# Attention b: weighted values in quadrants and in two parts, with copies and exponentials in another order

## The chip, the cores and the metric

The kernel runs on one core of a Trainium2 chip. The metric is device time of one execution in microseconds (us), the median of three runs. PE is TensorE, DVE VectorE, ACT ScalarE, POOL GpSimd.

## The reference, cut to what matters

Four layers with residuals: attention a, a mixture of experts (FFN), attention b, and the FFN again. Inputs are 8 batches of 256 positions by 128 features, all in float32. The change is in attention b:

```
Q, K, V = per head (16 heads of 64) from the normalised x
scores  = Q K^T, masked so that a query sees only keys up to itself
attn    = softmax(scores / 8)
z       = attn V            # the weighted values
out     = z_flat W_O^T      # x = x + out
```

## The kernel before, in words

Attention b goes in 32 steps of one software pipeline: 8 batches with 4 steps each (j = 0 to 3), each step two pairs of heads (x = 0, 1; in a pair hh = 0, 1). A pair is two heads of 64, so q and k of a pair fill 128 partitions. Every engine runs its own `step(b, j)`; order is fixed by hand in the code, and engines wait for each other by semaphores. In step n = (b, j), with n1 the next step and n2 the one behind it:

- PE (`step` in `tensor`): scores of n1 for both pairs (`scores_b`), transposes of the weights of n (`turn_p(n, 0)`), q and k of n2 (`project_qk(n2, 0)`), V (`project_v`), `turn_p(n, 1)`, `project_qk(n2, 1)`, some work for the next FFN layer (`turn_v`, `affinity`, `rank`), at j = 1 the next batch's input turned (`turn_xb`), at j = 0 the output projection of the last batch (`out_proj_b`), and weighted values of n (`values_b`).
- DVE: copy of the values out of PSUM (`copy_z`), reciprocal of the softmax sums (`invert(n, 1)`), maxima of n1's scores (`max_b`, four to a pair, which also write the masked scores to SBUF), copies of q and k (`copy_qk`), a copy of transposed weights (`copy_p`), `invert(n1, 0)`, and small work for the FFN layer.
- ACT: copies of transposed weights (`copy_p`, three of the four that a step has), exponentials (`exp_b`), a copy of V (`copy_v`).
- POOL: multiplies the exponentials by the reciprocals (`divide`).

PSUM is `ps`, 8 banks of 512 columns. Banks 0 to 3 hold the scores, `jb` (bank 4) q and k of a projection, `bank[0]` and `bank[1]` (5, 6) the transposed weights, `bank[2]` (7) V and the weighted values. The queries of the second 128 stand in swapped halves of 64 (`QUERIES`), so that score matmuls on both column halves of PE are nearly even. Such a matmul has 64 rows (one head) and 64 columns (64 queries) of the array: a quadrant. A values matmul before the change has all 128 rows (keys) and 64 columns:

```
last = nc.tensor.matmul(bank[2][hh * DHB:(hh + 1) * DHB, x * L + kt * P:(x + 1) * L],
                        vb[:, v:v + DHB], pT[:, c:c + L - kt * P], start=kt == 0,
```

In the profile L1007 is scores, L1040 `turn_p`, L965 `project_qk`, L972 `project_v`, L1053 `values_b`, L982 `out_proj_b`, L956 `turn_xb`; on DVE L1454 `copy_z`, L1478 `invert`, L1468 `max_b`, L1449 `copy_qk`, L1458 `copy_p`; on ACT L696 `exp_b`, L704 `copy_p`, L709 `copy_v`. A float32 matmul shows as two records. An exponential or maximum shows as the instruction and a read of its accumulator.

Of the kernel before, what the change touches and what calls it, by code (L numbers as in the profile page):

```python
# [48 lines left out]
QUERIES = ((0, 1), (3, 2))  # L49

# [43 lines left out]
def constants():  # L94
# [6 lines left out]
    k = np.arange(L)  # L101
    for t, at, n in ((0, C_CAUSAL, P), (1, C_LATE, L)):
        q = HALF * np.array(QUERIES[t])[r // HALF] + r % HALF
        c[:, at:at + n] = np.where(k[None, :n] > q[:, None], MASKED, 0.0)
# [57 lines left out]
def hybrid_layer(nc, x_in, w_a, wo_a, b_a, bo_a, w_b, wo_b, cent, w1, w2, b2, sel_in, const, out):  # L162
    ctx = ExitStack()
    with ctx:
# [6 lines left out]
        def sems(prefix, names):  # L171
# [115 lines left out]
        (b_w, b_xn, b_xT, b_xTs, b_j, b_qk, b_vp, b_v, b_s, b_mx, b_e, b_r, b_n, b_t, b_pa, b_pd, b_pv,  # L287
         b_z, b_o, b_x) = sems("b_", "w xn xT xTs j qk vp v s mx e r n t pa pd pv z o x")
# [21 lines left out]
        jb = wide[:, 4 * 512:5 * 512]  # L310
        wb_ = [wide[:, i * 512:(i + 1) * 512] for i in range(5)]
        aff_at = ((2 * 512, 6 * 512, 2 * 512, 6 * 512), (5 * 512, 5 * 512, 5 * 512, 0, 2 * 512))
# [245 lines left out]
        def _(act):  # L558
# [81 lines left out]
            def turned_v(k, g):  # L640
                act.wait_ge(f_vT, k * NG + g + 1)
                need(act, f_aff, k * NG + g)
                n = GROUPS[k][g][1]
                nc.scalar.copy(vTt[:, 0:n * P], bank[k][:, 0:n * P]).then_inc(f_vTs, 1)
# [45 lines left out]
            def exp_b(n, x, heads=(0, 1)):  # L690
                act.wait_ge(b_mx, 2 * nth(n) + x + 1)
                for hh in heads:
                    for t in range(T):
                        o, m = p_at(n, x, hh, t), m_at(n, x) + t * 2 + hh
                        px = pb[:, o:o + (t + 1) * P]
                        last = nc.scalar.activation(px, px, ACT.Exp, bias=nmax[:, m:m + 1], scale=-1.0, accum_out=psum[:, m:m + 1])  # L696
# [3 lines left out]
            def copy_p(n, x, hh):  # L700
# [3 lines left out]
                nc.scalar.copy(pT[:, c:c + BLOCKS * P], bank[hh][:, 0:BLOCKS * P]).then_inc(b_pa, 1)  # L704
# [6 lines left out]
            def step(b, j):  # L711
                n, n1 = (b, j), at(b, j + 1)
                bv = b + j // 2
                if ok(n):
                    copy_p(n, 0, 1)
                    copy_p(n, 0, 0)
                if ok(n1):
                    exp_b(n1, 0, [0])
# [4 lines left out]
                if ok(n1):  # L723
                    exp_b(n1, 0, [1])
# [17 lines left out]
        def _(pe):  # L742
# [105 lines left out]
            def turn_v(k, g):  # L848
# [3 lines left out]
                for i in range(n):  # L852
                    t = lo + i
                    last = nc.tensor.transpose(bank[k][:, i * P:(i + 1) * P], pack[:, t * ROW:t * ROW + D], ident)
# [97 lines left out]
            def turn_xb(b):  # L952
                pe.wait_ge(b_xn, b + 1)
                need(pe, b_pa, 3 * STEPS * b - 6)
                for t in range(T):
                    last = nc.tensor.transpose(bank[1][:, t * P:(t + 1) * P], xn[:, t * D:(t + 1) * D], ident)  # L956
                last.then_inc(b_xT, 1)

            def project_qk(n, x):
                need(pe, b_qk, 2 * nth(n) + x)  # L960
                if n[1] == 0:
                    pe.wait_ge(b_xTs, n[0] + 1)
                for i in range(2):
                    c = i * HB * DHB + (2 * n[1] + x) * P
                    last = nc.tensor.matmul(jb[:, i * L:(i + 1) * L], wb[:, c:c + P], xnT[:, 0:L], start=True, stop=True)  # L965
# [20 lines left out]
            def out_proj_last(lo, hi):  # L986

                pe.wait_ge(b_qk, 2 * NB * STEPS)
                pe.wait_ge(b_z, NB * STEPS - STEPS + (hi + 1) // 2)
                for p in range(lo, hi):  # L990
                    for t in range(T):
                        last = nc.tensor.matmul(jb[:, t * P:(t + 1) * P], zT[:, p * L + t * P:p * L + (t + 1) * P],
# [5 lines left out]
            def scores_b(n, x):  # L998
# [3 lines left out]
                for t in range(T):  # L1002
                    for half, q in enumerate(QUERIES[t]):
                        for hh in range(2):
                            rows, n = slice(hh * DHB, (hh + 1) * DHB), (q + 1) * HALF
                            c = (2 * x + hh) * 512 + t * P
                            last = nc.tensor.matmul(wide[half * HALF:(half + 1) * HALF, c:c + n],  # L1007
                                                    qk[rows, r + q * HALF:r + (q + 1) * HALF],
                                                    qk[rows, r + L:r + L + n],
                                                    start=t == 0, stop=t == T - 1, skip_group_check=True)  # L1010
                if x == 1:
                    last.then_inc(b_s, 1)

            def turn_p(n, x):
                pe.wait_ge(b_n, 2 * nth(n) + x + 1)
                for hh in (1, 0):
# [19 lines left out]
                    for c in range(BLOCKS):  # L1036
                        o = p_at(n, x, hh, c)
                        to = bank[hh][:, 0:P] if c == 0 else \
                            view(wide, (5 + hh) * 512 + c * P + HALF, [[-HALF, 2], [1, HALF]])
# [3 lines left out]
            def values_b(n):  # L1043
                pe.wait_ge(b_pa, 3 * nth(n) + 3)
                pe.wait_ge(b_pd, nth(n) + 1)
# [543 lines left out]
```

## Time and profile before

| | us |
|---|---|
| median of 3 runs | 521.23 (521.12 to 521.76) |
| profiled execution, whole | 525.47 |
| its span | 523.7 |
| busy in the span: PE, DVE, ACT, POOL | 433.5, 360.2, 264.8, 237.9 |
| attention b, about | 190 to 449 in the span |

Busy time says how long an engine had something running. Which engine sets the time of a stage is read from who waits for whom there; an engine's idle time costs nothing as long as others don't wait for it. The chain of the profile is followed back from the last instruction.

### The profile page before, as it was taken

The page shows a single profiled execution, that of the slowest core. Times are in us where ns is not written, and L with a number is a line of the kernel's source. Part 1 is how long each engine was busy: PE and PEld are TensorE (multiplying, and loading weights), DVE is VectorE, ACT ScalarE, POOL GpSimd, SP SyncE. Part 2 cuts the span into 40 slices and gives each one's busy share as a digit, 9 for nine tenths or more (in the row PEclk, how much of TensorE's full clock was granted, in tenths as well). Part 3 has the DMA queues.
Part 4 walks back from the last instruction along what each step waited for, and adds up shares of the span by engine and source line. Part 5 has one row for each costly group of instructions (what it writes and reads, how often), then busy time and mean ns, then how long its engine had stood idle before and what let it go on. Part 6 is the DMA issues. An engine that isn't in the chain of part 4 may idle for free.

```text
span 523.7 us, 11678 instructions
## 1 busy us (share of the span) xinstructions
PE 433.5 (83%) x3890; PEld 340.8 (65%) x3890; DVE 360.2 (69%) x1417; ACT 264.8 (51%) x928; POOL 237.9 (45%) x251
## 2 busy tenths in 40 slices
PE   2847989622999388999999999999999998439993
PEld 1324557522999346777787777777787787339992
DVE  6689996723656358867768688786878766446661
ACT  1641036500545127767758678576774857115450
POOL 6100789452445415533436335473455546314453
PEclk9997899555999879999999999999999999759997
DMA  8999930024655200000000000000000000136640
GB/s 313 363 393 421 420 144 0 32 91 121 200 172 160 63 29 1 3 1 1 3 1 3 2 2 11 12 22 1 2 12 11 22 1 22 42 101 199 199 139 5
DMA packets 22234, 48.98 MB, mean 94 GB/s; under 512 B 3328, under 2 KB 13574, under 8 KB 19744
## 3 DMA queue, kind: packets, MB, share of 16 engines
q1 hardware_dynamic: 18880, 40.86, 22.2%
q0 software_dynamic: 3296, 7.39, 4.5%
q8 instruction: 32, 0.52, 0.4%
q14 instruction: 26, 0.21, 0.2%
HBM read 24.99 MB, written 24.15 MB: 94 GB/s over the span
## 4 chain that ended last, share of the span: by engine, by line
PE 62%; DVE 13%; POOL 9%; issue 6%; DMA 4%; ACT 3%; another core or an unknown queue 2%; POOLq 0%; SPq 0%; DVEq 0%; ACTq 0%
PE ps L965 9%; PE ps L909 8%; PE ps L922 7%; PE ps L1040 7%; PE ps L1053 7%; PE ps L1007 6%; PE ps L972 4%; PE ps L982 4%; POOL sum L468 3%; POOL vT L531 2%; PE ps L755 2%; ACT vT L696 2%; DVE prod L1151 2%; POOL sum L476 1%
## 5 line engine op out<-in xcount | busy, mean ns | idle before, releaser
L531 POOL TENSOR_TENSOR vT<-vT,prec 128x256 f32<-128x256 f32 (+1 forms) x128 | 103.2, 827 | 128.3 <-DVE prec L1478 127.3
L696 ACT ACTIVATE vT<-vT,nmax 128x128 f32<-128x128 f32 (+1 forms) x256 | 113.4, 449 | 12.0 <-DVE nmax L1468 11.9
L1468 DVE CUSTOM_DVE_ANT_0 vT<-ps,cst 128x128 f32<-128x128 f32 (+1 forms) x256 | 77.5, 350 | 6.8 <-PE ps L1007 6.7
L704 ACT COPY prod<-ps 128x384 f32<-128x384 f32 x96 | 42.9, 482 | 60.5 <-PE ps L1040 60.5
L965 PE MATMUL ps<-xnT,wb 128*128 128x256 f32 x256 | 67.3, 386 | 1.4 <-DVE qk L1449 0.9
L1040 PEld LDWEIGHTS ps<-cst,vT 128*128 128x128 f32 x384 | 42.8, 141 | 30.2 <-issue 16.7
L1040 PE MATMUL ps<-cst,vT 128*128 128x128 f32 x384 | 54.5, 278 | 4.0 <-POOL vT L531 2.9
L1449 DVE COPY qk<-ps 128x512 f32<-128x512 f32 x64 | 43.4, 678 | 13.7 <-PE ps L965 13.5
L922 PE MATMUL ps<-w2s,pv 128*128 (+1 forms) x368 | 49.3, 277 | 1.4 <-ACT pv L669 0.8
L965 PEld LDWEIGHTS ps<-xnT,wb 128*128 128x128 f32 x256 | 44.5, 193 | 7.5 <-DVE qk L1449 2.4
L696 ACT ACTIVATION_READ_ACCUMULATOR vT<-vT,nmax 128x1 f32 x256 | 49.3, 192 | 0.0
L1053 PE MATMUL ps<-prod 128*64 128x256 f32 (+1 forms) x512 | 48.7, 332 | 0.1
L922 PEld LDWEIGHTS ps<-w2s,pv 128*128 128x128 f32 x368 | 45.0, 193 | 2.5 <-issue 2.4
L1007 PE MATMUL ps<-qk 64*64 64x64 f32 (+3 forms) x1024 | 42.6, 303 | 0.8 <-DVE qk L1449 0.7
L501 POOL DMA_INDIRECT sorted_in<-pack,row x32 | 31.8, 993 | 24.6 <-DVE pack L1321 17.4
L1053 PEld LDWEIGHTS ps<-prod 128*64 128x64 f32 x512 | 32.0, 136 | 15.3 <-issue 5.4
L468 POOL TENSOR_TENSOR sum<-pv 128x1024 f32<-128x1024 f32 x8 | 18.9, 2357 | 40.0 <-DVE pv L1195 39.3
L508 POOL DMA_INDIRECT out<-pv,dest x23 | 22.6, 983 | 31.7 <-DVE pv L1389 19.9
L508 POOL DMA_INDIRECT after_ffn<-pv,dest x23 | 22.8, 990 | 31.3 <-DVE pv L1389 23.0
L1007 PEld LDWEIGHTS ps<-qk 64*64 64x64 f32 x1024 | 30.3, 133 | 7.7 <-DVE qk L1449 4.2
L669 ACT ACTIVATE pv<-ps,pv 128x128 f32<-128x128 f32 x60 | 18.8, 364 | 30.3 <-PE ps L909 27.6
L972 PE MATMUL ps<-wb,xnT 128*128 128x512 f32 x64 | 33.9, 612 | 0.1
(158 smaller groups left out, 794.6 us busy)
## 6 DMA issues: line engine op xcount, KB each, us to landing
sorted_in<-zero SPq DMA_DIRECT2D x1, 16512.0 KB, 64.8
pv<-in_w SPq DMA_DIRECT2D x30, 259.0 KB
pv<-sorted_in SPq DMA_DIRECT2D x46, 129.0 KB
wps<-in_w SPq DMA_DIRECT2D x1, 2072.0 KB, 9.5
w2s<-in_w SPq DMA_DIRECT2D x1, 2048.0 KB, 13.8
wb<-in_w_b SPq DMA_DIRECT2D x1, 1536.0 KB, 22.6
xres<-in_x SPq DMA_DIRECT2D x4, 256.0 KB, 4.1
xres<-in_bo_a POOLq DMA_DIRECT2D x2, 512.0 KB, 13.0
```

Of the source, the lines that this page charges most:

```text
L508: nc.gpsimd.indirect_dma_start(out=place, out_offset=bass.IndirectOffsetOnAxis(ap=dest[q][:, 0:1], axis=0), in_=ys[q][:], in_offset=None, ...
L531: last = nc.gpsimd.tensor_tensor(px, px, view(prec, m_at(n, x) + t * 2, [[1, 2], [0, (t + 1) * P]]), ALU.mult)
L696: last = nc.scalar.activation(px, px, ACT.Exp, bias=nmax[:, m:m + 1], scale=-1.0, accum_out=psum[:, m:m + 1])
L704: nc.scalar.copy(pT[:, c:c + BLOCKS * P], bank[hh][:, 0:BLOCKS * P]).then_inc(b_pa, 1)
L922: last = nc.tensor.matmul(wide[:, s % 2 * 512:s % 2 * 512 + D], hT[s % 2][:, c * P:(c + 1) * P], w, start=c == 0, stop=c == FC - 1)
L965: last = nc.tensor.matmul(jb[:, i * L:(i + 1) * L], wb[:, c:c + P], xnT[:, 0:L], start=True, stop=True)
L972: nc.tensor.matmul(bank[2][:], xnT[:, i % 2 * P:(i % 2 + 1) * P], wb[:, c:c + 512], start=True, stop=True).then_inc(b_vp, 1)
L1007: last = nc.tensor.matmul(wide[half * HALF:(half + 1) * HALF, c:c + n], qk[rows, r + q * HALF:r + (q + 1) * HALF], qk[rows, r + L:r + L + ...
L1040: last = nc.tensor.transpose(to, pb[:, o:o + P], ident)
L1053: last = nc.tensor.matmul(bank[2][hh * DHB:(hh + 1) * DHB, x * L + kt * P:(x + 1) * L], vb[:, v:v + DHB], pT[:, c:c + L - kt * P], start=k ...
L1449: nc.vector.tensor_copy(qk[:, r:r + 2 * L], jb).then_inc(b_qk, 1)
L1468: ins = nc.vector.tensor_tensor_reduce(out=pb[:, o:o + w], in0=wide[:, c:c + w], in1=cst[:, mask:mask + w], scale=-1.0, scalar=-MASKED * 2 ...
```

## The change

Weighted values (`values_b`) are made in quadrants. A matmul now has 64 keys as rows. For each 64 keys only the queries from them on are columns, so 256, 192, 128 or 64. The two row halves of PE write to two banks: in part 0 the lower half works on pair 0 and the upper on pair 1, in part 1 the other way round. Part 0 stays at the end of a step; part 1 stands in the next step between the scores of the two pairs, behind a wait (`b_ph`) for part 0. For that the keys of the second 128 are stored in swapped halves too (`turn_xb`, the masks, `scores_b`), and scores of one query block take two matmuls, 128 and 64 keys, instead of one of 192. The scores signal after each pair (`b_s`).

PSUM is given out anew: values in banks 6 and 7, transposed weights in 4 and 5, q and k of pair 0 in bank 6 and of pair 1 in bank 3 (`later`), behind the maxima that read it. DVE copies the values behind the first maximum, and `copy_p` stands behind all maxima, ahead of `invert(n1, 0)`. ACT's exponentials of n1's first head stand ahead of the copies of weights, and those of the second head ahead of the V copy.

```diff
             def values_b(n, part):
+                if part == 0:
+                    pe.wait_ge(b_pa, 3 * nth(n) + 3)
+                    pe.wait_ge(b_pd, nth(n) + 1)
+                    pe.wait_ge(b_v, least(nth(n) + 3, NB * STEPS))
+                    if ok(at(n[0], n[1] + 2)):
+                        pe.wait_ge(b_qk, 2 * nth(n) + 5)
+                    need(pe, b_z, nth(n))
+                else:
+                    pe.wait_ge(b_ph, nth(n) + 1)
+                for kt in range(T):
+                    for r in range(2):
+                        x, k, rows = r ^ part, QUERIES[kt][r], slice(r * HALF, (r + 1) * HALF)
                         for hh in range(2):
-                            c = (2 * x + hh) * BLOCKS * P + kt * 2 * P
+                            c = (2 * x + hh) * BLOCKS * P + kt * 2 * P + k % 2 * HALF
...
+                            last = nc.tensor.matmul((bank[1], bank[2])[x][hh * DHB:(hh + 1) * DHB, k * HALF:L],
+                                                    vb[rows, v:v + DHB], pT[rows, c:c + L - k * HALF],
...
+                last.then_inc((b_ph, b_pv)[part], 1)
```

```diff
             def project_qk(n, x):
-                need(pe, b_qk, 2 * nth(n) + x)
+                if x == 0:
+                    if nth(n) > 2:
+                        pe.wait_ge(b_z, nth(n) - 2)
+                    else:
+                        need(pe, b_qk, 2 * nth(n) - 1)
+                else:
+                    need(pe, b_mx, 2 * nth(n))
+                    need(pe, b_qk, 2 * nth(n))
```

PE's `step`:

```diff
                 if ok(n1):
                     scores_b(n1, 0)
+                if ok(at(b, j - 1)):
+                    values_b(at(b, j - 1), 1)
+                if ok(n1):
                     scores_b(n1, 1)
...
                 if ok(n):
-                    values_b(n)
+                    values_b(n, 0)
```

ACT's `step`:

```diff
+                if ok(n1):
+                    exp_b(n1, 0, [0])
                 if ok(n):
                     copy_p(n, 0, 1)
                     copy_p(n, 0, 0)
                 if ok(n1):
-                    exp_b(n1, 0, [0])
+                    exp_b(n1, 0, [1])
                 if some(bv) and j != 1 or some(b) and j == 1:
                     copy_v(n, (j + 2) % STEPS)
                 if ok(n):
                     copy_p(n, 1, 1)
                 if ok(n1):
-                    exp_b(n1, 0, [1])
                     exp_b(n1, 1)
```

DVE's `step`:

```diff
-                if ok(at(b, j - 1)):
-                    copy_z(at(b, j - 1))
                 if ok(n):
                     invert(n, 1)
                 if ok(n1):
-                    scored(n1)
+                    scored(n1, 0)
+                    max_b(n1, 0, 0, 0)
+                if ok(at(b, j - 1)):
+                    copy_z(at(b, j - 1))
...
+                if ok(n):
+                    copy_p(n)
                 if nth(n) == LAST:
                     choose(1, due("affinity", n))
-                if ok(n):
-                    copy_p(n)
                 if ok(n1):
-                    max_b(n1, 1, 1, 1)
                     invert(n1, 0)
+                if ok(n2):
+                    copy_qk(n2, 1)
                 if j == 1 and some(b + 1):
                     copy_xT(b + 1)
-                if ok(n2):
-                    copy_qk(n2, 1)
```

How this moves instructions is seen at three places.

ACT, one step in the middle of attention b, before. `prod<-ps 128x384` is a copy of transposed weights, `prod<-ps 128x512` the V copy, `vT,psum<-vT,nmax` an exponential:

```order
L704 COPY prod<-ps 128x384 x2
L696 ACTIVATE vT,psum<-vT,nmax 128x128
L696 ACTIVATE vT,psum<-vT,nmax 128x256
L709 COPY prod<-ps 128x512
L704 COPY prod<-ps 128x384
L696 ACTIVATE vT,psum<-vT,nmax 128x128
L696 ACTIVATE vT,psum<-vT,nmax 128x256
```

The same step after the change:

```order
L702 ACTIVATE vT,psum<-vT,nmax 128x128
L702 ACTIVATE vT,psum<-vT,nmax 128x256
L711 COPY prod<-ps 128x384 x2
L702 ACTIVATE vT,psum<-vT,nmax 128x128
L702 ACTIVATE vT,psum<-vT,nmax 128x256
L716 COPY prod<-ps 128x512
L711 COPY prod<-ps 128x384
```

Each head's exponentials of the first pair have moved ahead of the copies that they stood behind. In both, the four exponentials of the second pair follow.

DVE, the start of a step (values' copy `prod<-ps 128x512`, reciprocal, then maxima, each an `ISA` row with a read of the accumulator), before:

```order
L1454 COPY prod<-ps 128x512
L1478 RECIPROCAL prec<-psum 128x4
L1468 ISA vT,nmax<-ps,cst 128x128
L1468 ISA nmax 128x1
L1468 ISA vT,nmax<-ps,cst 128x256
L1468 ISA nmax 128x1
```

and after:

```order
L1508 RECIPROCAL prec<-psum 128x4
L1498 ISA vT,nmax<-ps,cst 128x128
L1498 ISA nmax 128x1
L1484 COPY prod<-ps 128x512
L1498 ISA vT,nmax<-ps,cst 128x256
L1498 ISA nmax 128x1
```

The copy of the values now stands behind the reciprocal and one maximum.

PE, the end of a step and the start of the next (values `ps<-prod`, scores `ps<-qk`), before:

```order
L1053 MATMUL ps<-prod 64x256 x2
L1053 MATMUL ps<-prod 64x128 x2
L1053 MATMUL ps<-prod 64x256 x2
L1053 MATMUL ps<-prod 64x128 x2
L1007 MATMUL ps<-qk 64x64 x2
L1007 MATMUL ps<-qk 64x128 x2
L1007 MATMUL ps<-qk 64x256 x2
L1007 MATMUL ps<-qk 64x192 x2
```

and after, from the scores of the first pair on (the four rows of part 0, like those of part 1, stand ahead):

```order
L1027 MATMUL ps<-qk 64x64 x2
L1027 MATMUL ps<-qk 64x128 x2
L1027 MATMUL ps<-qk 64x256 x2
L1027 MATMUL ps<-qk 64x128 x2
L1027 MATMUL ps<-qk 64x64 x2
L1078 MATMUL ps<-prod 64x256 x2
L1078 MATMUL ps<-prod 64x192 x2
L1078 MATMUL ps<-prod 64x64 x2
L1078 MATMUL ps<-prod 64x128 x2
L1027 MATMUL ps<-qk 64x64 x2
L1027 MATMUL ps<-qk 64x128 x2
```

The second part of the values has come in between the scores of the two pairs, and a pair's scores have a row more.

## Rows read from the trace of the kernel before

**Rows 1.** The page's span, and busy time of each engine from 200 to 440 us.

```profile
span 523.7 us, 11678 instructions
...
core 0: us, PE busy (x) PEld busy (x) DVE busy (x) ACT busy (x) POOL busy (x), PEclk, DMA share, GB/s
200.00:440.00 240.00, 236.84 (x2408) 182.25 (x2407) 185.18 (x817) 168.09 (x620) 113.12 (x135) 1.00 0.02 6
```

**Rows 2.** Chain that ended last, four steps: start us, us, engine, tile, line, records.

```profile
306.56 1.25 PE ps L1007 x23
...
311.86 1.45 PE ps L1053 x16
313.31 1.25 PE ps L1007 x23
314.56 0.81 PE ps L1040 x6
...
317.09 0.66 PE ps L1040 x6
317.74 0.87 PE ps L965 x4
...
325.56 3.69 PE ps L982 x32
...
335.99 0.22 PE ps L956 x2
```

**Rows 3.** Timeline of PE at the start of a step: start us, us, operation.

```profile
298.63 1.32 PE L1007 MATMUL ps<-qk 64*64 64x64 f32 x32
```

**Rows 4.** Timeline of DVE, the same columns, and idle time before with its releaser.

```profile
300.02 0.29 DVE L1468 CUSTOM_DVE_ANT_0 vT<-ps,cst 128x128 f32<-128x128 f32 x1 [0.50 <-PE ps L1007]
...
307.09 0.68 DVE L1454 COPY prod<-ps 128x512 f32<-128x512 f32 x1
307.69 0.17 DVE L1478 RECIPROCAL prec<-psum 128x4 f32<-128x4 f32 x1
...
308.10 0.42 DVE L1468 CUSTOM_DVE_ANT_0 vT<-ps,cst 128x256 f32<-128x256 f32 x1
...
309.00 0.08 DVE L1468 DVE_READ_ACCUMULATOR2_ANT nmax<- 128x1 f32 x1
...
310.68 0.29 DVE L1468 CUSTOM_DVE_ANT_0 vT<-ps,cst 128x128 f32<-128x128 f32 x1
...
311.03 0.56 DVE L1458 COPY prod<-ps 128x384 f32<-128x384 f32 x1
...
312.25 0.18 DVE L1478 RECIPROCAL prec<-psum 128x4 f32<-128x4 f32 x1 [0.33 <-ACT vT L696]
...
314.67 0.16 DVE L1478 RECIPROCAL prec<-psum 128x4 f32<-128x4 f32 x1
314.75 0.26 DVE L1468 CUSTOM_DVE_ANT_0 vT<-ps,cst 128x128 f32<-128x128 f32 x1
```

**Rows 5.** Timeline of ACT in one step, the same columns.

```profile
308.32 0.86 ACT L704 COPY prod<-ps 128x384 f32<-128x384 f32 x2 [2.21 <-PE ps L1040]
309.12 0.40 ACT L696 ACTIVATE vT<-vT,nmax 128x128 f32<-128x128 f32 x1
...
310.38 0.59 ACT L709 COPY prod<-ps 128x512 f32<-128x512 f32 x1 [0.26 <-PE ps L972]
310.86 0.48 ACT L704 COPY prod<-ps 128x384 f32<-128x384 f32 x1
311.23 0.41 ACT L696 ACTIVATE vT<-vT,nmax 128x128 f32<-128x128 f32 x1
...
312.02 0.20 ACT L696 ACTIVATION_READ_ACCUMULATOR vT<-vT,nmax 128x1 f32 x1
312.12 0.39 ACT L696 ACTIVATE vT<-vT,nmax 128x128 f32<-128x128 f32 x1
...
313.78 0.19 ACT L696 ACTIVATION_READ_ACCUMULATOR vT<-vT,nmax 128x1 f32 x1
```

More of the change, by code:

```diff
@@ L643, in turned_v @@
                 n = GROUPS[k][g][1]
-                nc.scalar.copy(vTt[:, 0:n * P], bank[k][:, 0:n * P]).then_inc(f_vTs, 1)
+                nc.scalar.copy(vTt[:, 0:n * P], turn_ps[k][:, 0:n * P]).then_inc(f_vTs, 1)
             def exps(k, g):
@@ L703, in copy_p @@
                 c = (2 * x + hh) * BLOCKS * P
-                nc.scalar.copy(pT[:, c:c + BLOCKS * P], bank[hh][:, 0:BLOCKS * P]).then_inc(b_pa, 1)
+                nc.scalar.copy(pT[:, c:c + BLOCKS * P], turn_ps[hh][:, 0:BLOCKS * P]).then_inc(b_pa, 1)
             def copy_v(n, i):
@@ L853, in turn_v @@
                     t = lo + i
-                    last = nc.tensor.transpose(bank[k][:, i * P:(i + 1) * P], pack[:, t * ROW:t * ROW + D], ident)
+                    last = nc.tensor.transpose(turn_ps[k][:, i * P:(i + 1) * P], pack[:, t * ROW:t * ROW + D], ident)
                 last.then_inc(f_vT, 1)
@@ L964, in project_qk @@
                     c = i * HB * DHB + (2 * n[1] + x) * P
-                    last = nc.tensor.matmul(jb[:, i * L:(i + 1) * L], wb[:, c:c + P], xnT[:, 0:L], start=True, stop=True)
+                    last = nc.tensor.matmul((bank[1], later)[x][:, i * L:(i + 1) * L], wb[:, c:c + P], xnT[:, 0:L],
+                                            start=True, stop=True)
                 last.then_inc(b_j, 1)
@@ L1003, in scores_b @@
                     for half, q in enumerate(QUERIES[t]):
[L1004 to L1012, printed above, removed]
+                        for lo, hi in KEYS[q]:
+                            for hh in range(2):
+                                rows, at_q = slice(hh * DHB, (hh + 1) * DHB), r + (t * 2 + half) * HALF
+                                c = (2 * x + hh) * 512 + t * P
+                                last = nc.tensor.matmul(
+                                    wide[half * HALF:(half + 1) * HALF, c + lo * HALF:c + hi * HALF],
+                                    qk[rows, at_q:at_q + HALF], qk[rows, r + L + lo * HALF:r + L + hi * HALF],
+                                    start=t == 0, stop=t == T - 1, skip_group_check=True)
+                last.then_inc(b_s, 1)
             def turn_p(n, x):
@@ L1056, in values_b @@
-                last.then_inc(b_pv, 1)
+                            last = nc.tensor.matmul((bank[1], bank[2])[x][hh * DHB:(hh + 1) * DHB, k * HALF:L],
+                                                    vb[rows, v:v + DHB], pT[rows, c:c + L - k * HALF],
+                                                    start=kt == 0 and part == 0, stop=kt == T - 1 and part == 1,
+                                                    skip_group_check=True)
+                last.then_inc((b_ph, b_pv)[part], 1)
@@ L1448, in copy_qk @@
                 dve.wait_ge(b_j, 2 * nth(n) + x + 1)
-                nc.vector.tensor_copy(qk[:, r:r + 2 * L], jb).then_inc(b_qk, 1)
+                nc.vector.tensor_copy(qk[:, r:r + 2 * L], (bank[1], later)[x]).then_inc(b_qk, 1)
             def copy_z(n):
```

57 lines of the change are left out of this document (29 added, 28 removed).

## Prediction, made before the changed kernel ran

> **What bounds the kernel now.** I read the windows first. From 200 to 440 us, nearly all of attention b, PE is busy 236.84 of 240 us at granted clock 1.00, its 2.4 GHz level, while DVE has 185.18, ACT 168.09 and POOL 113.12 [rows 1]. Then the chain. It stays on PE through a whole step, and the start of the scores comes again after 313.31 - 306.56 = 6.75 us [rows 2]. The reader should see that the pieces (values 1.45, scores 1.25, transposes 0.81 and 0.66, two q/k projections of 0.87, a V projection of like length) fill the 6.75 us with no wait. So attention b costs what PE issues. An output projection adds 3.69 once in four steps (j = 0), and turning the next batch's input adds 0.22 (j = 1) [rows 2]. A batch takes 4 x 6.75 + 3.69 + 0.22 = 30.91 us.
>
> The other engines follow at their own distance. Step lengths alone don't show that, so I read one step of ACT [rows 5] and of DVE [rows 4]. I call E0 ACT's start on the exponentials of the next step's first head pair.
>
> **What PE gains.** A q/k projection of two 256-column matmuls takes 0.87 us, 1.69 ns a column [rows 2]. Values are now two heads side by side, 2 x (256 + 128) = 768 columns: 1.29 of the 1.45; the other 0.16 is the change of tile shape at its ends. In quadrants, each row half streams 256 + 64 or 192 + 128 = 320 columns in a part: 0.54, two parts 1.08. Scores already run in quadrants: 64 + 256 and 128 + 192 make 320 columns a head pair, so 1.08 for both and 0.17 for the change of shape, of 1.25 [rows 2]. The cut of the 192-column key range into 128 + 64 adds four matmuls and no column. Its cost isn't in the trace; nothing to 4 x 0.05 = 0.2 us bounds it (a 64-column matmul is two passes of 0.05), and I take nothing, since the scores' present 64-column matmuls fit their columns. Scores and values together fall from 2.70 to 4 x 0.54 + 0.17 = 2.33: PE alone would go from 6.75 to 6.38 a step.
>
> The Trainium skill, TensorE: Matmul & The Clock Gate, "The mechanism", says that matmuls start and end in strict program order. By it a wider matmul in one quadrant would hold back a later one in another, and a score pair would last 128 + 256 = 384 columns, 0.65 us. The row speaks against it: two such pairs would be 1.30 without the change of shape, and the row has 1.25 with it [rows 2].
>
> **What ACT and DVE now wait for.** All times are from the start of the first scores, T.
>
> - First maximum: in the trace it starts at 300.02, 1.39 after scores from 298.63, of which 1.08 is columns [rows 3, 4]. So 0.31 passes from the last column to DVE. In the changed kernel the first pair alone is awaited: 0.54 + 0.31 = 0.85.
> - Copy of the values: it needs the second part, which ends on PE at 0.54 + 0.54 = 1.08, so it starts at 1.39. It occupies DVE for 307.69 - 307.09 = 0.60 before the next starts. Three more maxima take 308.10 to 309.08 = 0.98. ACT follows 0.04 later at 309.12 [rows 4, 5]. E0 = 1.39 + 0.60 + 0.98 + 0.04 = **3.01**. Before, the same exponentials start 309.12 - 306.56 = 2.56 after the scores, and the two copies of transposed weights (308.32) have gone ahead of them by then [rows 2, 5].
> - ACT now has, in order: E0's two exponentials 0.89, two copies 0.80, the second head's exponentials 0.89, the V copy 0.48, the last copy of weights 0.48 to its end. These are start to start 312.12 - 311.23 for a head, 309.12 - 308.32 for two copies, 310.86 - 310.38 for the V copy [rows 5]. Together 3.54. Only then may PE begin the first part of the values, which waits for all copies of the weights. With 0.05 to PE (near DVE's 0.04 to ACT) and 0.54 for the part, the next T is E0 + 4.13. Before, the last copy ended at 311.34, and PE wanted it at 311.79: 0.45 slack. Now PE would be ready at 6.38 - 0.54 = 5.84, and gets it at 3.01 + 3.59 = 6.60.
> - There is a second ring, without PE. After the last copy ACT has four exponentials of the second pair: 0.37 to their start, then 1.85 (312.12 to 313.97) [rows 5]. They end at E0 + 3.06 + 0.37 + 1.85 = E0 + 5.28. DVE's reciprocal of them stands at the head of its next step, ahead of the first maximum. It starts 0.03 after ACT ends (312.22 to 312.25); the maximum 0.08 behind it (314.67 to 314.75), the values' copy 0.35 behind that (310.68 to 311.03), then 0.60, 0.98 and 0.04 again: 2.08 [rows 4, 5]. The ring is 5.28 + 2.08 = **7.36 us**. Before, ACT's two copies ran while DVE worked on the maxima; now they stand inside the ring.
>
> Queued behind E0 are the copies that PE's second transposes need (same PSUM banks): 3.01 + 0.89 + 0.86 + 0.05 = 4.81, and PE is ready for the second of them at about 6.38 - 0.54 - 0.87 - 0.33 = 4.6. This is inside the later wait, except at j = 0.
>
> Step by step in a batch: j = 0 has room for everything behind 3.69 us of output projection, but not for the transposes: with E0 at 3.23, the copies end at 4.98, 0.05 to PE and half of the 0.66 for transposes bring 5.36, then projection 0.87, output 3.69, part 0.54: 10.5 (before 10.44). j = 1 starts clean: 3.01 + 4.13 + 0.22 = 7.36, the turn of the input being behind the same copy (before 6.97). j = 2: the exponentials end 3.01 + 5.28 - 7.36 = 0.93 after T, E0 = 3.01, 7.14 (6.75). j = 3: they end at 1.15, E0 = 3.23, 7.36 (6.75). Sum 32.36 against 30.91: **+1.45 a batch**. Seven whole batches (steps 2 to 29) give 10.2. The steps before and the last two are chains of waits already; the last gain a little on PE and lose on ACT. I take +0.9 for them, of 0 to +2.
>
> Other edits at nothing: projections into other banks. The one into the scores' last bank waits for all maxima, at 3.2 + 1.1 = 4.3; PE reaches it at 5.3. Were the cover gone, its lateness would fall on every step. DVE's copy of weights follows PE's transposes (5.3 + 0.3 + 0.56 = 6.2), before the values may start at 6.6.
>
> Sum: the profiled execution has a span of 523.7 and 525.47 in all, 0.8% above the median of the plain runs, 521.23. 525.47 + 11.1 = 536.6, and by that ratio **532.3 us**.
>
> **The rivals.** A bound for both signs: within 0.2% (1 us) a measurement can't tell.
>
> 1. *The rings close as computed*: 532.3, its own range 527 to 537. 0.68.
> 2. *Faster: ACT keeps up*, and PE's 0.37 is kept over some 30 steps: 521.23 - 11 = 510. The place is E0. It decides if E0 starts at 5.84 - 3.59 = 2.25 or sooner instead of 3.01. For it: the first maximum comes half a microsecond sooner, and ACT is busy only 70% now. Against: the copy of the values can't start before 1.39 on any row here. The Trainium skill, TensorEngine Tiling (Array Packing), "PSUM Bottleneck", warns that tiling speeds TensorE but not the emptying of PSUM; no row of before shows it, for PE is the bound there. 0.14.
> 3. *Only the ring through PE binds*, the second being opened by a shorter handover than I read: the three j > 0 steps then cost about 6.9 to 7.1 and the total is 523 to 526. 0.08.
> 4. *More than that*: matmuls hold to strict order (the rule above: 0.65 for 0.54). Then the copy of the values starts at 1.61, E0 at 3.23, the part ends 0.11 later. Steps of 7.68, 7.45, 7.45 and 10.6 are +2.3 a batch, 538. Or DVE's batches of other work (gating of the next layer), which now stand in a ring with no slack, add 0.9 us in several steps: 536 to 541. 0.10 together.
>
> **Numbers.** The lower end reaches into case 3 and the upper into case 4: 523 to 540 leaves out case 2, part of 3 and the tail of 4, 0.2. Faster is case 2 and a corner of 3, 0.15; same 0.03; slower 0.82.
>
> **What the profile after should show.** The scores' period in steps j = 2, 3 above 7 us. PE idle ahead of the values (and a little ahead of the second transposes), released by ACT's copy. ACT's E0 about 3.0 to 3.2 after the first scores, ended by DVE's maximum, and ACT idle only there, about 2 us a step. The first reciprocal of a DVE step released by ACT. PE's scores and values together at 2.3 us when unstalled. Wrong if PE has no wait there, if E0 stands below 2.3, or if a values part lasts 1 us, which would mean that quadrants of two row halves don't run side by side.

## The result, and the profile after

The changed kernel takes 531.72 us (median of 4 runs, 530.99 to 532.21) against 521.5 for the kernel before: ratio 1.0193, 95% interval 1.0173 to 1.0214. It is slower by 1.9%, 10.2 us; 532.3 had been forecast.

The two profiled executions differ by 5.7 us in span (523.7 [rows 1] and 529.4). That of before was a long one, 4 us above its median, and it lost this ahead of attention b: V's first projection stands at 186.9 us there and at 182.0 after. From that matmul to the first FFN matmul behind attention b it is 281.1 us before and 291.1 after: 10.0 us, as the medians say. All of it is in attention b.

Busy time after, from 200 to 440 us, which answers to [rows 1]:

```profile
core 0: us, PE busy (x) PEld busy (x) DVE busy (x) ACT busy (x) POOL busy (x), PEclk, DMA share, GB/s
200.00:440.00 240.00, 226.78 (x3035) 182.79 (x3030) 174.73 (x785) 157.89 (x598) 109.39 (x130) 1.00 0.02 6
```

PE was busy 236.84 of these 240 us; now it is idle for 13, at the same granted clock. The waits of 200 to 450 us say for whom (engine, line, released by: us in all, times, longest):

```profile
ACT vT L702 <- DVE nmax L1498: 84.4, 30, 5.9
...
DVE prec L1508 <- ACT vT L702: 10.8, 13, 1.4
PEld ps L1078 <- ACT prod L711: 7.5, 12, 0.7
...
PE ps L1058 <- ACT prod L711: 4.4, 18, 0.4
...
PEld ps L982 <- DVE prod L1484: 2.4, 4, 0.9
```

In the kernel before, the row that answers to the first is:

```profile
ACT vT L696 <- DVE nmax L1468: 7.7, 10, 1.5
```

ACT's exponentials (L702) now stand idle for DVE's maxima (L1498) once in every step, about 2.8 us each; DVE's reciprocal waits for ACT; PE's values (L1078) and transposes (L1058) wait for ACT's copies (L711). PEld is the load of the stationary operand, which goes ahead of each matmul.

One step on ACT, which answers to [rows 5] (start us, us, operation, idle before and releaser):

```profile
309.20 0.40 ACT L702 ACTIVATE vT<-vT,nmax 128x128 f32<-128x128 f32 x1 [2.59 <-DVE nmax L1498]
...
310.10 0.84 ACT L711 COPY prod<-ps 128x384 f32<-128x384 f32 x2
310.83 0.41 ACT L702 ACTIVATE vT<-vT,nmax 128x128 f32<-128x128 f32 x1
...
311.72 0.57 ACT L716 COPY prod<-ps 128x512 f32<-128x512 f32 x1
312.18 0.48 ACT L711 COPY prod<-ps 128x384 f32<-128x384 f32 x1
312.55 0.41 ACT L702 ACTIVATE vT<-vT,nmax 128x128 f32<-128x128 f32 x1
...
316.36 0.40 ACT L702 ACTIVATE vT<-vT,nmax 128x128 f32<-128x128 f32 x1 [1.83 <-DVE nmax L1498]
```

From the last of ACT's exponentials to the first of the next step, on DVE ([rows 4]):

```profile
314.46 0.18 DVE L1508 RECIPROCAL prec<-psum 128x4 f32<-128x4 f32 x1 [0.32 <-ACT vT L702]
314.56 0.26 DVE L1498 CUSTOM_DVE_ANT_0 vT<-ps,cst 128x128 f32<-128x128 f32 x1
...
314.74 0.69 DVE L1484 COPY prod<-ps 128x512 f32<-128x512 f32 x1
...
315.34 0.41 DVE L1498 CUSTOM_DVE_ANT_0 vT<-ps,cst 128x256 f32<-128x256 f32 x1
```

And PE in the same stretch ([rows 2]):

```profile
312.72 0.77 PE L1078 MATMUL ps<-prod 64*64 64x256 f32 x16 [0.30 <-ACT prod L711]
...
313.31 0.73 PE L1027 MATMUL ps<-qk 64*64 64x64 f32 x20
...
313.86 0.72 PE L1078 MATMUL ps<-prod 64*64 64x256 f32 x16
...
314.41 0.73 PE L1027 MATMUL ps<-qk 64*64 64x64 f32 x20
...
315.07 0.88 PE L1058 MATMUL ps<-cst,vT 128*128 128x128 f32 x6
```

The reader should see both rings closed. ACT starts at 309.20 and again at 316.36, a period of 7.16 us in which it works without a gap until 314.4 and then waits for reciprocal, maximum, copy and three maxima. PE's values at 312.72 start 0.06 after ACT's last copy ends at 312.66. ACT's start E0, forecast 3.01 after the first scores, is 316.36 - 313.31 = 3.05. PE itself got what it was promised: part 0, scores, part 1, scores follow at 0.59, 0.55, 0.55 and 0.66, 2.35 us for what took 2.70.

Lengths of a step without extra work, from one V projection to the next:

| step | before | forecast | after |
|---|---|---|---|
| j = 0 (output projection) | 10.43 | 10.5 | 10.46 |
| j = 1 (input turned) | 6.97 | 7.36 | 7.50 |
| j = 2 | 6.75 | 7.14 | 7.08 |
| j = 3 | 6.75 | 7.36 | 7.16 |
| batch | 30.90 | 32.36 | 32.20 |

And the sum by stretches: from V of step -2 to V of step 2 it is 27.5 us before and 28.8 after, on to V of step 29 216.6 and 224.1, from there to the FFN 36.5 and 37.8. That is +1.3, +7.5 and +1.3. (Here and below this last stretch, called the end, is counted from the second record of that V projection, 0.43 us after its first.)

### The profile page after: what moved, and what is told of

Same layout as the page of the kernel before. It is cut to its first block, busy times and chain, and to the rows that moved or that the text cites. A ratio compares the mean times of both kernels' runs of the same rounds, so it can differ in the third digit from the quotient of the medians.

```text
span 529.4 us, 13238 instructions
## 1 busy us (share of the span) xinstructions
PE 432.0 (82%) x4658; PEld 349.9 (66%) x4658; DVE 357.2 (67%) x1417; ACT 260.0 (49%) x928; POOL 237.7 (45%) x251
## 4 chain that ended last, share of the span: by engine, by line
PE 42%; DVE 20%; ACT 17%; POOL 9%; issue 7%; DMA 3%; POOLq 0%; SPq 0%; ACTq 0%; DVEq 0%
ACT vT L702 11%; PE ps L917 8%; PE ps L930 8%; DVE vT L1498 5%; PE ps L1000 5%; POOL sum L474 4%; PE ps L982 3%; ACT prod L711 3%; PE ps L1058 3%; DVE prod L1484 3%; PE ps L1078 3%; POOL sorted_in L507 2%; POOL sum L482 2%; PE ps L763 2%; PE ps L1027 2%
## 5 line engine op out<-in xcount | busy, mean ns | idle before, releaser
L702 ACT ACTIVATE vT<-vT,nmax 128x128 f32<-128x128 f32 (+1 forms) x256 | 114.4, 455 | 90.4 <-DVE nmax L1498 90.4
L1498 DVE CUSTOM_DVE_ANT_0 vT<-ps,cst 128x128 f32<-128x128 f32 (+1 forms) x256 | 75.0, 350 | 1.6 <-PE ps L1027 1.5
L982 PE MATMUL ps<-xnT,wb 128*128 128x256 f32 x256 | 68.4, 391 | 3.4 <-DVE nmax L1498 1.4
L1058 PEld LDWEIGHTS ps<-cst,vT 128*128 128x128 f32 x384 | 40.7, 140 | 32.6 <-issue 28.8
L1058 PE MATMUL ps<-cst,vT 128*128 128x128 f32 x384 | 55.0, 279 | 6.2 <-ACT prod L711 4.9
L1078 PEld LDWEIGHTS ps<-prod 64*64 64x64 f32 x1024 | 43.8, 133 | 12.5 <-ACT prod L711 8.2
L1078 PE MATMUL ps<-prod 64*64 64x256 f32 (+3 forms) x1024 | 48.0, 303 | 3.8 <-ACT prod L711 3.4
L702 ACT ACTIVATION_READ_ACCUMULATOR vT<-vT,nmax 128x1 f32 x256 | 50.5, 197 | 0.0
L1027 PE MATMUL ps<-qk 64*64 64x64 f32 (+2 forms) x1280 | 46.8, 271 | 0.1
L1027 PEld LDWEIGHTS ps<-qk 64*64 64x64 f32 x1280 | 43.9, 134 | 1.3 <-issue 0.8
L711 ACT COPY prod<-ps 128x384 f32<-128x384 f32 x96 | 42.2, 472 | 1.3 <-PE ps L1058 1.3
L507 POOL DMA_INDIRECT sorted_in<-pack,row x32 | 31.8, 994 | 22.2 <-DVE pack L1351 14.7
L1488 DVE COPY prod<-ps 128x384 f32<-128x384 f32 x32 | 17.8, 558 | 25.1 <-PE ps L1058 25.1
```

The source lines that it names most:

```text
L507: nc.gpsimd.indirect_dma_start(out=xs_dram, out_offset=bass.IndirectOffsetOnAxis(ap=row[:, t:t + 1], axis=0), in_=pack[:, t * ROW:(t + 1) ...
L711: nc.scalar.copy(pT[:, c:c + BLOCKS * P], turn_ps[hh][:, 0:BLOCKS * P]).then_inc(b_pa, 1)
L982: last = nc.tensor.matmul((bank[1], later)[x][:, i * L:(i + 1) * L], wb[:, c:c + P], xnT[:, 0:L], start=True, stop=True)
L1058: last = nc.tensor.transpose(to, pb[:, o:o + P], ident)
L1078: last = nc.tensor.matmul((bank[1], bank[2])[x][hh * DHB:(hh + 1) * DHB, k * HALF:L], vb[rows, v:v + DHB], pT[rows, c:c + L - k * HALF], s ...
L1498: ins = nc.vector.tensor_tensor_reduce(out=pb[:, o:o + w], in0=wide[:, c:c + w], in1=cst[:, mask:mask + w], scale=-1.0, scalar=-MASKED * 2 ...
```

## The experiments

Ratios are to the kernel before on the same chip; chips differ by up to 4.7 us (the kernel before had medians of 520.9, 523.6 and 525.6 on three of them), so ratios are compared, not times. Each run has one profile, so a difference between stretches is one of single executions. "Clean step" is one with neither output projection, input turn nor gating work, from V projection to V projection.

**1. ACT's order of before in the changed kernel**

```diff
-                if ok(n1):
-                    exp_b(n1, 0, [0])
                 if ok(n):
                     copy_p(n, 0, 1)
                     copy_p(n, 0, 0)
                 if ok(n1):
-                    exp_b(n1, 0, [1])
+                    exp_b(n1, 0, [0])
...
                     copy_p(n, 1, 1)
                 if ok(n1):
+                    exp_b(n1, 0, [1])
                     exp_b(n1, 1)
```

> The changed kernel with ACT's order of before (two copies of transposed weights, first head's exponentials, V copy, last copy, second head's exponentials, second pair), all else as changed. Theory (two rings through ACT: the values wait for ACT's last copy, and DVE's next maxima wait for ACT's last exponential with the copies inside that ring): the copies leave both rings, the long ring falls from 7.16 to about 6.4 us, PE's own 6.38 is reached, a step without output projection takes 6.4 to 6.6, whole time 511 to 515. Rival (the new waits of the projections for maxima and banks, or the quadrant matmuls themselves, cost the time): no change from the changed kernel, 529 to 533, and PE's waits ahead of the projections stay or grow.

Measured: 524.01, ratio 1.0050 (1.0032 to 1.0068); steps 2 to 29 take 214.2 us. So ACT's order costs 1.4% of the 1.9%. But 511 to 515 was wrong: a clean step is 6.67, not 6.4. Steps 2 to 29 already cost 2.4 us less than in the kernel before (216.6); the loss is ahead of them (28.8 for 27.5) and in the end (39.1 for 36.5), where PE waits 1.92 us for maxima ahead of the last output projection. Two steps of its timeline (PE L981 q/k projection, L989 V; ACT L716 V copy; DVE L1507 reciprocal, L1497 maximum, L1483 copy of the values):

```profile
248.38 1.13 PE L981 MATMUL ps<-xnT,wb 128*128 128x256 f32 x4
...
249.35 1.02 PE L989 MATMUL ps<-wb,xnT 128*128 128x512 f32 x2
...
250.41 0.59 ACT L716 COPY prod<-ps 128x512 f32<-128x512 f32 x1 [0.16 <-PE ps L989]
...
254.03 0.18 DVE L1507 RECIPROCAL prec<-psum 128x4 f32<-128x4 f32 x1 [0.99 <-ACT vT L702]
254.13 0.26 DVE L1497 CUSTOM_DVE_ANT_0 vT<-ps,cst 128x128 f32<-128x128 f32 x1
...
254.31 0.69 DVE L1483 COPY prod<-ps 128x512 f32<-128x512 f32 x1
...
255.05 1.13 PE L981 MATMUL ps<-xnT,wb 128*128 128x256 f32 x4
```

This is a third ring, which the prediction had not named. The q/k projection of pair 0 and the values of pair 0 now share bank 6. The projection starts 0.05 after the copy of the values ends (255.00); V follows, ACT's V copy waits for V, six exponentials stand behind it, DVE's reciprocal behind them, and the copy behind that: 255.05 - 248.38 = 6.67.

**2. ACT's new order alone, in the kernel before**

```diff
+                if ok(n1):
+                    exp_b(n1, 0, [0])
                 if ok(n):
...
                 if ok(n1):
-                    exp_b(n1, 0, [0])
+                    exp_b(n1, 0, [1])
...
-                    exp_b(n1, 0, [1])
```

> The kernel before with ACT's new order alone: values on 128 rows, banks, DVE's and PE's order as before. Theory: exponentials start 2.56 after the scores as before, the last copy of weights ends 3.54 later at 6.10 where it ended at 4.8, the values begin at 6.15 and not 5.30, so a step takes 7.6 and a batch 33.8 for 30.9: about 542. The ring without PE is 6.6 there and doesn't bind. Rival (the order of ACT is harmless and the loss is from quadrants, banks or DVE's order): 521 to 523.

Measured: 543.45, ratio 1.0411 (1.0373 to 1.0449). Clean steps take 7.59 and a batch 34.1 (10.90, 8.02, 7.59, 7.59). PE's timeline names ACT twice a step, ahead of the second transposes and of the values:

```profile
248.54 0.85 PE L1041 MATMUL ps<-cst,vT 128*128 128x128 f32 x6 [0.28 <-ACT prod L704]
249.22 1.03 PE L966 MATMUL ps<-xnT,wb 128*128 128x256 f32 x4
250.56 1.52 PE L1054 MATMUL ps<-prod 128*64 128x256 f32 x16 [0.31 <-ACT prod L704]
252.01 1.32 PE L1008 MATMUL ps<-qk 64*64 64x64 f32 x32
```

The order costs more without quadrants than with them, since each step then has PE's 1.45 us of values in the ring instead of 0.54.

**3. The copy of the values behind four maxima**

```diff
                     max_b(n1, 0, 0, 0)
+                    max_b(n1, 0, 0, 1)
+                    for t in range(T):
+                        max_b(n1, 0, 1, t)
                 if ok(at(b, j - 1)):
                     copy_z(at(b, j - 1))
                 if ok(n1):
-                    max_b(n1, 0, 0, 1)
-                    for t in range(T):
-                        max_b(n1, 0, 1, t)
```

> The changed kernel with DVE's copy of the values behind all four maxima of the first pair and not behind the first one; ACT's order as changed. Theory: exponentials start at about 2.1 to 2.4 after the scores and not 3.0 to 3.2, both rings lose the copy's 0.6, the ring without PE is 6.55, steps of 6.4 to 6.6 with perhaps 0.2 of PE's wait ahead of the first projection, which needs the copy: 512 to 517. Rival (ACT's order alone costs it, the copy's place doesn't matter): 528 to 532. Rival (quadrants or banks cost it): 529 to 533.

Measured: 529.31, ratio 1.0175 (1.0123 to 1.0228). A miss as a time: the clean steps fell to 6.73, as both rings through ACT should, but the copy is now late for PE, which the expectation had at 0.2 us a step:

```profile
PEld ps L982 <- DVE prod L1484: 19.8, 29, 1.8
PE ps L982 <- DVE prod L1484: 12.0, 16, 1.6
```

Steps with gating work on DVE ahead of the copy lose most (8.23 at step 11, 7.70 in the change). The two places can't be told apart as a whole: 1.0175 here and 1.0193 in the change, with intervals that overlap. Either way the copy is in a ring, ACT's behind the first maximum and PE's behind the fourth; it is the bank plan that makes it urgent for PE.

**4. Only the first head's exponentials ahead of the copies**

```diff
                     copy_p(n, 0, 1)
                     copy_p(n, 0, 0)
-                if ok(n1):
-                    exp_b(n1, 0, [1])
...
                     copy_p(n, 1, 1)
                 if ok(n1):
+                    exp_b(n1, 0, [1])
                     exp_b(n1, 1)
```

> The changed kernel with the second head's exponentials back behind the V copy and the last copy of weights; the first head's stay ahead of the copies. The ring without PE has the same work in it and stays 7.16, the ring through the values loses 0.89. Theory of two rings: the steps drift to the long ring (6.6, 6.8, 7.2, 11.2 in a batch), a little faster than changed, 526 to 530. Rival, only the values' wait for the last copy counts: PE's 6.38 is reached, 511 to 515.

Measured: 535.75, ratio 1.0268 (1.0229 to 1.0308). The steps of a clean batch are 10.66, 6.91, 7.10 and 7.15, near the 31.8 expected in sum. ACT's period is still that of the long ring:

```profile
244.06 0.40 ACT L702 ACTIVATE vT<-vT,nmax 128x128 f32<-128x128 f32 x1 [1.93 <-DVE nmax L1497]
...
251.21 0.40 ACT L702 ACTIVATE vT<-vT,nmax 128x128 f32<-128x128 f32 x1 [1.93 <-DVE nmax L1497]
```

251.21 - 244.06 = 7.15. So the rival, that only PE's wait for the last copy counts, falls. The time of 526 to 530 was missed: steps with gating work grew (8.41 at step 11 for 7.70) and the end took 41.1 us for 37.8. In the end PE's clock fell too (0.82 over 442 to 448 us), and the 16 records of the last output projection took 3.65 us for 2.02.

**5. The reciprocal behind the copy of the values, with ACT's order of before**

```diff
-                if ok(n):
-                    invert(n, 1)
                 if ok(n1):
                     scored(n1, 0)
                     max_b(n1, 0, 0, 0)
                 if ok(at(b, j - 1)):
                     copy_z(at(b, j - 1))
+                if ok(n):
+                    invert(n, 1)
```

> The changed kernel with ACT's order of before and, on DVE, the reciprocal of the second pair behind the copy of the values and not at the step's head. In the run with ACT's order alone a clean step took 6.67 us, along a third ring: PE's first q/k projection waits for the copy of the values (same bank 6), V follows it, ACT's V copy and last copy, its six last exponentials, DVE's reciprocal, a maximum, the copy. If that ring is the cause, a clean step now falls to PE's own 6.4, a batch from 30.1 to 29.5, and the whole to 517 to 521; steps with DVE's gating work stay late by their own. If something else holds the 6.67 (matmuls in quadrants cost more, or waits for maxima), nothing moves: 523 to 525.

Measured: 522.77, ratio 1.0021 (0.9998 to 1.0044), above the 517 to 521 expected. Clean steps are 6.43, so the third ring is shown, and PE's own pace of 6.4 with it:

```profile
247.91 1.02 PE L989 MATMUL ps<-wb,xnT 128*128 128x512 f32 x2
...
250.38 0.78 PE L1077 MATMUL ps<-prod 64*64 64x256 f32 x16
250.97 0.73 PE L1026 MATMUL ps<-qk 64*64 64x64 f32 x20
251.53 0.72 PE L1077 MATMUL ps<-prod 64*64 64x256 f32 x16
252.07 0.73 PE L1026 MATMUL ps<-qk 64*64 64x64 f32 x20
...
254.34 1.02 PE L989 MATMUL ps<-wb,xnT 128*128 128x512 f32 x2
```

Steps 2 to 29 take 212.8 us, 3.8 less than before, and not 10: the steps with gating work hold up the copy. And the end takes 40.6 for 36.5, which gives it back.

**6. The reciprocal behind the copy alone** (the same diff in the changed kernel)

> The changed kernel with that reciprocal behind the copy of the values and all else as changed, ACT's order too. The ring without PE is opened (its maxima no longer wait for ACT's last exponential), the ring through the values and ACT's last copy stays: 3.0 + 4.13 = 7.1 a step. Theory of two nearly equal rings: no gain to speak of, 528 to 533. Rival, the ring without PE alone holds the changed kernel: steps of 6.7 or less, 518 to 524.

Measured: 534.33, ratio 1.0256 (1.0232 to 1.0279). The ring without PE is open: DVE's reciprocal (250.39) no longer stands ahead of the maximum at 249.26, which PE's scores release. The steps stay 7.13, by PE's wait for ACT's last copy:

```profile
247.84 0.77 PE L1078 MATMUL ps<-prod 64*64 64x256 f32 x16 [0.30 <-ACT prod L711]
```

Either ring through ACT alone gives 7.1 us; opening one is worth nothing. A little above the expected 528 to 533: steps 19 and 25 (8.23 and 8.50 for 7.72 and 7.90) and the end (by 1.1 us) grew.

**7. Both parts of the values together**

```diff
                 if ok(n):
                     values_b(n, 0)
+                    values_b(n, 1)
```

with ACT's order of before, no part between the scores, and DVE's copy, then its reciprocal, at the head of its step.

> The changed kernel with ACT's order of before, the second part of the values directly behind the first (PE waits for the first part's end), and DVE's copy of the values at the head of its step as before. Quadrants, banks and the late copy of weights stay as changed. Theory: PE loses a wait of 0.2 to 0.3 between the parts, so values take about 1.45 as before; the copy is early and nobody waits for it. A clean step of 6.6 to 6.75 and 520 to 524 in all. Rival, banks and the late copy of weights cost by themselves: 526 or more, with waits ahead of the projections.

Measured: 525.96, ratio 1.0086 (1.0060 to 1.0112). Clean steps 6.72, as expected; values take 1.46 (252.12 to 253.58) as they did on 128 rows, and the scores 1.21 (253.58 to 254.79). So quadrants pay only with other work between the parts. Steps 2 to 29 take 216.0, like before; 525.96 was above the expected 524 and at the edge of the rival's 526, and most of the excess is in the end, 40.1 us for 36.5. The rival's sign, waits ahead of the projections, shows in four steps (3.3 us in all from 200 to 440 us) and, for the last output projection, in the end (1.6 us): what banks and the late copy of weights cost lies there and not in the clean steps.

**8. The last output projection later**

In the changed bank plan `out_proj_last` accumulates in the scores' bank 0 and waits for maxima. Here it stands at the end of step 30, on top of 5:

```diff
-                if nth(n) == LAST - 1:
-                    out_proj_last(0, 4)
                 if nth(n) == LAST:
...
                 if ok(n):
                     values_b(n, 0)
+                if nth(n) == LAST - 1:
+                    out_proj_last(0, 4)
```

> The kernel with ACT's order of before and the reciprocal behind the copy of the values, and further the first part of the last batch's output projection (16 matmuls) moved from the middle of step 30 to its end, behind the values. There it waited 1.92 us for maxima, since the changed kernel puts it into the scores' bank 0, and then ran 3.56 us instead of 2.02 at a lower granted clock, with step 30's second transposes queued behind it. Theory: this wait is why the end of attention b is some 4 us longer (40.6 for 36.5 us from the last V projection to the FFN's first matmul) though clean steps are at 6.43: the end falls to 37 to 39 us, and the whole to 518 to 520.5, faster than before or the same. Rival (the end is long for another reason): 522 to 523.5.

Measured: 526.63, ratio 1.0068 (1.0042 to 1.0095), where 518 to 520.5 was expected: no better than 5, and its end is longer, 43.3 us for 40.6. The wait has only moved to the transposes, and it is longer. PE's timeline and the granted clock (the last figure but two of a window):

```profile
434.58 1.54 PE L1057 MATMUL ps<-cst,vT 128*128 128x128 f32 x6 [2.69 <-POOL vT L537]
...
438.10 3.31 PE L1010 MATMUL ps<-wob,prod 128*128 128x128 f32 x16
```

```profile
430.00:436.00 6.00, 3.31 (x48) 2.73 (x40) 4.76 (x27) 2.91 (x12) 3.39 (x4) 0.83 0.01 3
436.00:442.00 6.00, 5.92 (x51) 5.10 (x50) 0.74 (x2) 3.68 (x16) 2.56 (x3) 0.60 0.12 44
442.00:448.00 6.00, 4.13 (x45) 3.42 (x42) 2.87 (x14) 1.54 (x4) 3.57 (x4) 0.97 0.12 43
```

Behind an idle stretch of 2.69 us the clock is at its lower level, 1.2 GHz, for much of the next six microseconds, and 16 records of the output projection take 3.31 us, 2.02 in the kernel before, at 1.00. The Trainium skill, TensorE: Matmul & The Clock Gate, "HAM oscillation — how this bites in real kernels", describes this: gaps in PE's work bring the clock down, and the next work starts slow. The trace agrees in kind; that a gap of this size doesn't always do so is seen at 11.

**9. DVE's normalisation under the output projection**

On top of 8, `norm(1, g)` of steps 11 and 19 moves into steps 12 and 20, ahead of `residual_b`, and PE's `turn_v` behind `out_proj_b`:

```diff
                 g = due("turn", n)
-                if g is not None:
+                if g is not None and j != 0:
...
                     out_proj_b(n)
+                g = due("turn", n)
+                if g is not None and j == 0:
+                    pe.wait_ge(b_pa, 3 * nth(n) + 3)
+                    turn_v(1, g)
...
+                g = due("powers", at(b, j - 1))
+                if g is not None and j == 0:
+                    norm(1, g)
                 if j == 0 and some(b - 1):
...
                 g = due("powers", n)
-                if g is not None:
+                if g is not None and j != 3:
                     norm(1, g)
```

> The same, and DVE's normalisation for the next FFN layer (2.5 us) moved at steps 11 and 19 from the step's end to behind the q/k copies of steps 12 and 20, where DVE waits for the output projection; PE's turn of its result behind that projection. Theory: in the kernel with the reciprocal moved, steps 11 and 12 cost 7.9 and 10.4 against 6.43 and 10.09 for the like of them without this work, since it holds up the copy of the values and with it PE's projection: about 1.5 us less at each of two places, 515 to 518. Rival (it is hidden now): no change against the previous kernel.

Measured: 523.91, ratio 1.0003 (0.9978 to 1.0027), against 1.0068 for 8: 2.7 us over the whole, and not the 515 to 518 expected. Step 11 falls from 7.88 to 6.44, step 12 goes from 10.41 to 10.64. The steps 2 to 29 now take 210.2, 6.4 less than before, and the end 42.8.

**10. The same move in the kernel before** (the diff of 9)

> The kernel before with the same move of the normalisation and nothing else. Its steps 11 and 12 cost 6.75 and 11.69 against 6.75 and 10.44: about 0.8 us less at each of two places (the turn's 0.43 stays), 519 to 520.5. It shows what the move is worth without quadrants.

Measured: 521.91, ratio 0.9971 (0.9955 to 0.9988). Step 12 falls from 11.69 to 10.98. The move is worth 0.3% without quadrants. (519 to 520.5 was expected; on this chip the kernel before has 523.62, and the gain of 1.7 us is of the size meant.)

**11. PE kept busy at the end**

On top of 9, with the output projection back in the middle of step 30:

```diff
+                if nth(n) == LAST - 1:
+                    pe.wait_ge(b_pa, 3 * nth(n) + 1)
+                    for i in range(8):
+                        nc.tensor.transpose(jb[:, BLOCKS * P:], ident, ident)
+                    out_proj_last(0, 4)
```

> The kernel with quadrants, ACT's order of before, the reciprocal behind the copy and the normalisation under the output projection, with the last batch's output projection back in the middle of step 30, and ahead of it 8 transposes of a constant into unused columns of bank 4, whose result nobody reads. In the two kernels before this one PE stood idle for 1.9 to 2.7 us there and its granted clock fell to 0.6 to 0.8 in the stretches behind, with output matmuls of 0.44 us for two where it was 0.25; the end of attention b took 40.6 to 43.3 us for 36.5 in the kernel before. Theory (idle time of PE brings the clock down and that costs the gain back): with the idle time filled, granted clock stays at 0.95 or more until 442 us, the end takes 37 to 38.5 us, and the whole 515 to 519 against about 521.5, faster than before by 0.5 to 1%. Rival (the end is long for its waits alone, the clock only follows): end of 40 us or more, 521 to 524.

Measured: 523.3 where the kernel before has 525.6, ratio 0.9950 (0.9928 to 0.9972). This version is faster than both kernels, at the lower end of the 0.5 to 1% expected. The clock holds for these twelve microseconds (0.89 over the six behind them):

```profile
430.00:436.00 6.00, 5.17 (x94) 4.63 (x85) 5.47 (x30) 3.23 (x13) 3.65 (x5) 1.00 0.01 3
436.00:442.00 6.00, 4.75 (x60) 4.00 (x59) 1.51 (x4) 4.94 (x18) 4.57 (x6) 1.00 0.12 44
```

and 16 records of the output projection take 2.02 us again (L1010 at 434.61). The end took 39.0 us, 3.8 less than in 9 and above the 37 to 38.5 expected.

That the transposes kept the clock isn't shown, though. In 1 and in 5 PE stands idle for 1.92 us ahead of the same projection, and nothing fills the gap. The same six microseconds in 1, then in 5:

```profile
430.00:436.00 6.00, 4.08 (x86) 3.79 (x78) 5.49 (x30) 3.24 (x13) 4.20 (x5) 1.00 0.01 3
```

```profile
430.00:436.00 6.00, 4.08 (x23) 3.87 (x22) 3.56 (x21) 1.84 (x6) 3.61 (x4) 0.73 0.06 22
```

In 1 the clock stayed at 1.00, the projection started at 434.62 and took 2.02 us, and the end took 39.1, as here. In 5 the clock fell, the projection took 3.56, and the end took 40.6. So 1 against 5 gives the price of the lower clock in the end, 1.5 us, and 1 against 11 says that filling the gap gained nothing over a gap in which the clock held. What decides whether it holds stays open. The waits for maxima in the shared bank are what remains of the longer end.

Nor is all of the 0.5% from quadrants. The move of 9 is in it, and that alone gives the kernel before 0.3% (10): 0.9950 (0.9928 to 0.9972) against 0.9971 (0.9955 to 0.9988), with intervals that overlap. In the profiles the steps 2 to 29 take 210.3 us here and 215.2 in 10, so the quadrants with their bank plan save 4.9 us there, and the end gives back 3.1 (39.0 for 35.9). Whether anything is left of it as a whole isn't shown.

## Why the prediction was right, point by point

- **PE's gain**: 2.70 to 2.33 was forecast, 2.35 came, and 6.38 a step shows as 6.43 where nothing else binds (5). The cut of 192 keys into 128 + 64 costs nothing that can be seen: a score pair with its cut takes 0.55, by its columns 0.54. The strict order for matmuls in different quadrants (case 4) is refuted here: by the prediction's reckoning it would give 0.65. The row of before, which the prediction held against it, could not decide: 64, 128, 256 and 192 columns can start in the order of the code, two quadrants side by side, and still last 320. The values can, with 256, 192, 64 and 128: in the single records of the part at 312.72 a matmul of 128 columns starts at 313.11 and one of 64, which stands ahead of it in the code, at 313.20.
- **The ring through the values**: shown by 2 (there 7.6 forecast, 7.59 came) and 6 (7.13 for 7.14). ACT's 3.54 of work from the first exponential to the last copy's end is 3.46 after (309.20 to 312.66). In 2 the 2.56 from scores to exponentials is 2.63: it had been counted from the chain's 306.56, where the timeline has the scores at 306.49. The two small errors cancel.
- **The ring without PE**: shown by 4, which shortens the other ring and keeps 7.15. It was forecast at 7.36 and measures 7.16. The term that was too large is the step from maximum to copy, 0.35 taken from a maximum ahead of `copy_p`, 0.18 as measured; that row's copy had waited for its own input.
- **j = 1**: 7.36 forecast, 7.50 came. The turn of the input does wait behind ACT's copy (0.40 us, at 238.90), but from its start to the values, at 239.24, 0.34 pass, where 0.22 had been counted. That is 0.12 of the 0.14.
- **Sum**: +1.45 a batch was forecast, +1.30 came. The term "steps 2 to 29, +10.2" is too large: 7.5 up to V of step 29, since steps that were long before didn't get longer: 12, 13, 20 and 21, with gating work (11.51 and 7.81 for 11.69 and 7.86), and 26 and 27 (7.94 and 7.54 for 8.16 and 7.59). Against that, steps 11 and 19 grew by 0.95, more than their share. The term "ramp and end +0.9" is too small: +2.6. The two errors hide each other, and that 532.3 comes so near to 531.72 is luck; the 7.1 to 7.5 of a step is not.
- **What the sum called free and isn't**: "projections into other banks" were costed at nothing, with only the one into bank 3 weighed. That holds in the changed kernel, whose rings are slower (from 200 to 450 us the matmuls wait 1.4 us for that copy and their weight loads 2.4), but the one into bank 6 is the next bound: 1 and 5 show that it alone holds clean steps at 6.67, and every step with gating work pays for it. For that reason 1 and 5 stay far from rival 2's 510 even with ACT in order; the best version here gains 0.5%, the move of DVE's normalisation included.

## What to carry to other kernels

When one engine is the bound and another hands it work in every step, don't look at busy shares: write down the ring, from one start of an instruction to its next start, and sum what is on it. A reordering that starts one consumer earlier is free only for work that isn't ahead of another engine's wait. ACT was 70% busy before and 66% after, and set the pace.

If two orders each close a ring of the same length, opening one shows nothing (6), and a bank that is shared anew is a ring that only appears when the longer ones are gone (1). Test with both opened before calling a change bad: the quadrants did take a clean step from 6.75 to 6.43 us. And before crediting a change with a gain, give the old kernel the same side changes (10): most of the 0.5% may be theirs.

## What the runs showed of the hardware that was not expected

- Matmuls in different quadrants don't wait for each other's order: matmuls of 64 to 256 columns in four quadrants take the time of the fuller half, 320 columns, 0.55 us, and a later one of 128 columns starts 0.09 us ahead of an earlier one of 64.
- Around a run of quadrant work PE takes 0.05 us more at its start and 0.12 more at its end (0.59 and 0.66 where 0.54 is columns). It is put down to the change from a 128-row to a 64-row tile and back, which no run tests by itself.
- PE's granted clock fell behind an idle stretch of 1.92 us (to a mean of 0.73 over 430 to 436 us, in 5), of 1.83 (0.82 over 442 to 448, in 4) and of 2.69 (0.60 over 436 to 442, in 8), but not behind 1.92 us in 1, nor behind 1.60 in 7, both at 1.00. Idle stretches of 0.2 to 0.6 us in nearly every step, as in the changed kernel, left it at 1.00.
- The same 16 records take 2.02 us at 1.00 and 3.56 at the lower clock.
